# The prologue reordered: statistics of x after the second fold, the bias spread by a product with ones, and the guard's maxima before the statistics of batch 1

## The reference, cut to what matters

```python
def reference(x, Wq, Wk, Wv, Wo, bo, w_freq_real, w_freq_imag, bias):   # x is (8, 512, 256) f32
    def ffn(x):                                   # fft, product with a 256x256 complex matrix, real part of ifft
        y = real(ifft(einsum('bnd,do->bno', fft(x), w_freq_real + 1j * w_freq_imag)))
        return y + bias
    def attn(x):                                  # 16 heads of 8, on the left 128 columns of x
        left = x[..., :128]
        q, k, v = left @ Wq.T, left @ Wk.T, left @ Wv.T
        att = softmax(q . k / 4)                  # per head, over the keys
        return (att . v) @ Wo.T + bo
    x = x + 0.5 * ffn(layernorm(x))
    x = x + attn(layernorm(x))
    x = x + 0.5 * ffn(layernorm(x))
    return x
```

## Time and profile before

| what | value |
|---|---|
| median of 3 runs | 324.44 us (323.96 to 325.45) |
| span of the profiled execution | 327.4 us |
| granted TensorE clock, mean of the span | 0.995 |
| TensorE (PE) busy | 299.8 us, 92% |
| ScalarE (ACT) busy | 259.0 us, 79% |
| VectorE (DVE) busy | 190.3 us, 58% |
| GpSimd (POOL) busy | 97.8 us, 30% |
| first exponential of batch 0 starts at | 33.04 us |

### The profile page before, as it was taken

One profiled execution on the slowest core, in us unless ns is written; L12 is line 12 of the kernel. 1 busy time (PEld: TensorE's weight loads), 2 busy tenths in 40 slices (PEclk: granted clock), 3 DMA queues, 4 the chain that ended last, 5 costly groups with the idle time before them and its releaser, 6 DMA issues.

```text
span 327.4 us, 8919 instructions
## 1 busy us (share of the span) xinstructions
PE 299.8 (92%) x3452; PEld 113.8 (35%) x3452; DVE 190.3 (58%) x550; ACT 259.0 (79%) x287; POOL 97.8 (30%) x112
## 2 busy tenths in 40 slices
PE   8598999879998998999997999799997999898995
PEld 5444333233333432343332433233332323222333
DVE  1587438446775676657763677467764743361254
ACT  2114988978897988998995989878997999899921
POOL 6554701212504053033604053223600250034004
PEclk9999999999999999999997999999999999999999
DMA  7834459629654857748652858649354466303002
GB/s 200 298 132 171 104 202 173 175 86 139 209 201 135 188 107 256 225 147 147 237 182 70 188 105 289 193 140 151 114 163 146 102 180 167 109 28 103 35 32 66
DMA packets 29892, 49.87 MB, mean 152 GB/s; under 512 B 3600, under 2 KB 16272, under 8 KB 28944
## 3 DMA queue, kind: packets, MB, share of 16 engines
q1 hardware_dynamic: 29152, 48.79, 53.3%
q10 hardware_dynamic: 688, 0.40, 0.7%
HBM read 31.34 MB, written 17.83 MB: 150 GB/s over the span
## 4 chain that ended last, share of the span: by engine, by line
PE 57%; DMA 19%; SPq 9%; DVE 6%; issue 5%; ACT 3%; POOL 1%; DVEq 0%; ACTq 0%
PE misc L715 21%; PE ot L819 21%; PE scores L803 11%; DMA q_scr<-qp 7%; SPq L399 7%; DMA leftT<-left_scr 5%; DMA QS<-q_scr 4%; ACT probs L665 3%; DMA x_in<-x 2%; PE scores L715 1%; PE misc L689 1%; DVE stats L928 1%; DVE qp L972 1%; PE scores L682 1%; POOL rstd L547 1%
## 5 line engine op out<-in xcount | busy, mean ns | idle before, releaser
L665 ACT ACTIVATE probs<-scores 128x1024 f32<-128x1024 f32 x256 | 244.0, 1030 | 33.2 <-PE scores L803 33.0
L819 PE MATMUL ot<-probs,VS 128*32 128x512 f32 x1024 | 134.9, 598 | 4.8 <-ACT probs L665 3.4
L803 PE MATMUL scores<-QS,KS 32*128 32x512 f32 x512 | 65.0, 497 | 3.2 <-DMA QS<-q_scr 2.2
L803 PEld LDWEIGHTS scores<-QS,KS 32*128 32x128 f32 x512 | 24.6, 182 | 111.3 <-ACT probs L665 100.7
L819 PEld LDWEIGHTS ot<-probs,VS 128*32 128x32 f32 x1024 | 30.9, 110 | 28.4 <-ACT probs L665 7.7
L560 POOL TENSOR_TENSOR x_out<-x,half_bias 128x512 f32<-128x512 f32 x7 | 9.0, 1289 | 102.6 <-DVE x L1001 102.6
L1006 DVE SCALAR_TENSOR_TENSOR x_out<-misc,rstd,x_out 128x256 f32<-128x256 f32 x28 | 13.6, 484 | 38.7 <-PE misc L715 33.8
L545 POOL TENSOR_SCALAR veps<-mv 128x4 f32<-128x4 f32 (+1 forms) x25 | 5.9, 234 | 92.2 <-DVE mv L935 92.2
L715 PE MATMUL misc<-half_ffn,xT 128*32 128x256 f32 x448 | 32.1, 386 | 0.9 <-DMA xT<-x_scr 0.9
L715 PE MATMUL misc<-half_ffn,xT_in 128*32 128x256 f32 x400 | 27.7, 385 | 2.2 <-DVE half_ffn L1177 1.7
L547 POOL TENSOR_TENSOR rstd<-veps,power 128x4 f32<-128x4 f32 (+1 forms) x25 | 25.2, 1008 | 2.1
(11 more groups left out here) (126 smaller groups left out, 268.3 us busy)
## 6 DMA issues: line engine op xcount, KB each, us to landing
KS<-k_scr SPq DMA_DIRECT2D x56, 128.0 KB, 4.8
QS<-q_scr SPq DMA_DIRECT2D x56, 128.0 KB, 3.1
x_in<-x SPq DMA_DIRECT2D x8, 512.0 KB, 5.1
xT_in<-x_t SPq DMA_DIRECT2D x8, 512.0 KB, 6.5
k_scr<-kp SPq DMA_DIRECT2D x8, 512.0 KB, 2.7
q_scr<-qp SPq DMA_DIRECT2D x8, 512.0 KB, 4.6
x_scr<-x_blocks SPq DMA_DIRECT2D x7, 512.0 KB, 4.4
xT<-x_scr SPq DMA_DIRECT2D x7, 512.0 KB, 4.5
```

What stands on the lines that cost most here:

```text
L665: nc.scalar.activation(probs[u % PRING][:, :, :], scores[u % SRING][:, :, :], ACT.Exp, scale=SCORE_SCALE).then_inc(exp_done, 1)
L803: last = mm(scores[(u + j // 2) % SRING][:, j % 2, :], KS[b % 2][rows, slot, kt * P:(kt + 1) * P].bitcast(F32R), QS[b % 2][rows, slot, :]. ...
L819: last = mm(ot[COL * j:COL * (j + 1), :], VS[b % 2][:, kt, h, :], probs[(u + j // 2) % PRING][:, j % 2, :], start=s % 8 == 0, stop=s % 8 == 7)
```

## The change

The change touches only the prologue.

- VectorE: fold 2 no longer stands behind statistics of x. All four tiles' statistics of batch 0 come after fold 2; the memset of the cosine table's row comes right after fold 1.
- The bias is loaded first on ScalarE's queue, as one row of 256 into one partition. TensorE multiplies a row of 128 ones with it into a PSUM bank, ahead of piece 1. ScalarE makes `half_bias` from that bank, ahead of its copy of piece 1. The two tables are now second and third on ScalarE's queue.
- The fourth F1 of batch 1 is evacuated with the first three, ahead of KT and QT. The statistics and moments of batch 1 come after N and the chain that makes the flag, instead of between the evacuations and ahead of N.

```diff
-        jobs = [(f"F1_{t}", 1) for t in range(T)] + [("LT", 1)] + ahead[0:3] + [("KT", 1), ("QT", 1)] + ahead[3:4] + [("N", 1)]
+        jobs = [(f"F1_{t}", 1) for t in range(T)] + [("LT", 1)] + ahead + [("KT", 1), ("QT", 1), ("N", 1)]
...
-        bias_raw = sb("bias_raw", [P, E])
+        bias_raw = sb("bias_raw", [1, E])
+        ones_row = sb("ones_row", [1, P])
...
+        bias_bank = scores[2][:, 0, 0:E]
...
+            act.dma_start(bias_raw[:, :], bias.rearrange("(o e) -> o e", o=1)).then_inc(bias_loaded, 16)
             act.dma_start(cos_var_sb[:, :, :], cos_var.rearrange("(c p) e -> p c e", p=P)).then_inc(re_loaded, 16)
             act.dma_start(sin_sb[:, :, :], sin_tab.rearrange("(c p) e -> p c e", p=P)).then_inc(im_loaded, 16)
-            act.dma_start(bias_raw[:, :], bias.partition_broadcast(P)).then_inc(bias_loaded, 16)
...
+            act.wait_ge(bias_spread, 1)
+            nc.scalar.mul(half_bias[:, :], bias_bank, 0.5).then_inc(bias_set, 1)
             for piece, bank, copy in ((1, scores[0][:, 0], even[0]), (3, scores[1][:, 0], even[1])):
                 act.wait_ge(ffn_mm, piece)
                 nc.scalar.copy(copy[:, :, :], half_bank(bank)).then_inc(ffn_copied, 1)
-            act.wait_ge(bias_loaded, 16)
-            nc.scalar.mul(half_bias[:, :], bias_raw[:, :], 0.5).then_inc(bias_set, 1)
...
             pe.wait_ge(waking_set, 1)
             keep_awake(9)
+            pe.wait_ge(ones_set, 1)
+            pe.wait_ge(bias_loaded, 16)
+            mm(bias_bank, ones_row[:, :], bias_raw[:, :], start=True, stop=True).then_inc(bias_spread, 1)
             pe.wait_ge(re_loaded, 32)
...
             nc.vector.memset(waking[:, :].bitcast(I32), 0).then_inc(waking_set, 1)
+            nc.vector.memset(ones_row[:, :], 1.0).then_inc(ones_set, 1)
             nc.vector.memset(norms[:, :], 0.0).then_inc(norms_set, 1)
             fold(are_t, even[0], half_bank(scores[0][:, 1]), ALU.add, ALU.subtract, 2, 1)
-            norm0_stats(0, range(0, 2))
-
             dve.wait_ge(ffn_mm, 3)
             nc.vector.memset(cos_var_sb[0:1, 0, :], 1.0).then_inc(row0_set, 1)
             fold(aim_t, even[1], half_bank(scores[1][:, 1]), ALU.subtract, ALU.add, 4, 2)
-            norm0_stats(0, range(2, T))
+            norm0_stats(0)
             norm_moments(0, 1)
...
-            for s in range(T, T + 6):
-                run_jobs(PROLOGUE, s)
+            run_jobs(PROLOGUE, T)
+            for t in range(T):
+                evacuate(f"F1_{t}", 1)
+            run_jobs(PROLOGUE, 2 * T + 1)
+            run_jobs(PROLOGUE, 2 * T + 2)
             dve.wait_ge(row_ready, 1)
             nc.vector.tensor_copy(KS[0][:, 0, :].bitcast(F32R), row_banks[0]).then_inc(first_k_set, 1)
-            run_jobs(PROLOGUE, T + 6)
-            run_jobs(PROLOGUE, T + 7)
+            run_jobs(PROLOGUE, 2 * T + 3)
+            dve.wait_ge(evacuated, evac_count(f"F1_{T - 1}", 1))
+            for t in range(T):
+                norm_stats(1, x1[1], t, t == T - 1)
+            norm_moments(1, 2)
             guard(0)
```

More of the change, by code:

```diff
@@ L300, in build_macaron @@
         consts_set = sem("consts_set")
+        ones_set = sem("ones_set")
+        bias_spread = sem("bias_spread")
         bias_set = sem("bias_set")
```

## The result

The changed kernel is slower: 328.18 us median against 325.37 of the kernel before (20 runs each), ratio 1.0091 with a 95% interval of 1.0065 to 1.0118. A second comparison on another chip gave 1.0129 (1.0060 to 1.0198). The forecast was 322.2 us, a gain.

What follows compares the result with a forecast made beforehand. The body was taken as bound by a train of exponentials (244.0 of 327.4 us), only its start movable. Matrix stretch 1.95 - 0.9 = 1.05 plus guard stretch 1.14 gave 2.2 us: 324.44 - 2.2 = 322.2 us, range 321.0 to 324.2.

Steps and rivals of the forecast that it cites:

- D: Matrix stretch: delay of piece 4 by the bias product and later table issue, 0.9 us, leaving 1.95 - D as gain.
- The slower rival: ScalarE's queue: sine table lands 9.6 us after issue, at 11.4; D is 5.9, total 327.2 us; chance 0.08.
- The first rival: Engines serve 8 packets of x first: sine table lands at 7.4, D is 2.0, total 323.3 us; chance 0.12.
- The product: TensorE ahead of piece 1: the one-row bias product takes 0.45 us for 256 columns, a source of piece 4's delay.
- The 1.59 us of x: Matrix stretch: wait between pieces 4 and 5 for x and its first statistics, 1.59 us, expected to go.
- The 0.2 us to spare: Ahead of fold 3: VectorE's way with four statistics takes 2.5 us against TensorE's 2.68, so they are covered.
- The 0.36 us of fold 3: Matrix stretch: fold 3's first half gets 0.36 us shorter, as GpSimd's sum would be over earlier.
- The guard stretch: TensorE's flag load and branch move under the nine products of zeros, gaining the whole idle 1.14 us.
- the last rival: Batch borders in the body: if transfers don't follow, the gain is given back, 324.4 us; chance 0.09.

Runs made afterwards that it cites:

- after_again: The changed kernel, unchanged, for a second profile and timing on another chip; ratio 1.0129 against the kernel before.
- x_behind_tables: The changed kernel with x issued by SyncE only once wim and the sine table have landed; ratio 0.9981 against the kernel before.
- row_first_only: The kernel before with a load of one bias row, which nothing reads, put ahead of the tables on ScalarE's queue; ratio 1.0099 against it.
- guard_alone: The kernel before with only batch 1's job list, evacuation order and statistics place as changed; ratio 0.9973 against it.
- before_again: The kernel before, unchanged, for a second profile; F1 at 13.47 us, first exponential at 32.67, no ratio given.
- stats_guard: The kernel before with both VectorE reorderings and the bias left as a broadcast third on ScalarE's queue; 321.38 us against 323.06, ratio 0.9951.
- sin_on_sp: The changed kernel with the sine table's load moved to SyncE's queue, behind wim and ahead of x; ratio 0.9986 against the kernel before.
- bias_alone: The kernel before with only the bias part: row first, product ahead of piece 1, half_bias from PSUM; ratio 1.0150 against it.

## Why the prediction was wrong

- **The step that failed is D**, the delay of piece 4, taken as 0.9 us between the bounds 0.5 and 3.6. In the first profile it measured 4.82 us for piece 2's start and 2.06 more in pieces 2 to 4, 6.9 in all; in after_again 8.95 - 5.47 = 3.5, with none in the pieces. The upper bound was too low as well: it took x's landing as the latest at which the table could come, and the table landed at 10.25, after x (7.9) and after the transposed x (9.4), and in after_again at 8.91, after x (7.4). In place of two or three of x's packets in front of the table's last ones the runs show that about half of the tables' packets (272 of some 545 on that queue) were still to go when x's came, and that they took 5.9 us beside x, where the last 122 took 0.9 without it.
- **The term was sized by the issue time.** The sum treated "one place later" as 0.5 us of delay, with two or three of x's packets. x_behind_tables shows that 0.5 us of later issue is nothing alone (the table landed at 5.3), and row_first_only that the same 0.5 us beside x is 3.4 us of landing (8.8 instead of 5.4). A transfer without slack that loses its place to a large one doesn't lose the difference of the issue times.
- **The slower rival was the right one in kind.** It let the third transfer of the queue land 9.6 us after its issue; it was 8.5, and forecast 327.2 us against 328.18 measured (325.37 before). It was given 0.08, on the ground that the bias's packets were long and the table's short. That was beside the point: the long packets in the way were x's. That its loss of 2.8 us is the measured one is luck in part: its D of 5.9 has no clock in it, and D was 6.9 in one profile and 3.5 in the other.
- **The first rival**, the table behind a whole share of x, was too small: it put the table at 7.4 and the time at 323.3 us. Its mechanism is left open. The Trainium skill, "DMA: Bandwidth & Descriptors", Queues, rings and completion order, has an engine drain a group of descriptors of one ring before it switches. The counts in slices (35 and 4, later 17 and 79) come in bursts, which doesn't speak against it, but they can't show the order within one engine.
- **The clock was left out.** The prologue's idle times had cost no clock before, and the forecast never asked what a longer one would do. In the first profile the slow pieces are 2.06 of 4.19 us; in after_again there was none of it, with an idle time of 2.60 us.
- **The product** was put at 0.45 us and took 0.69 (0.62 on the chain), with piece 1 at 5.58 instead of 4.46; part of that is that the products of zeros ended later.
- **The 1.59 us of x** were right for that execution: the gap was 1.37 in the second profile and 0 in guard_alone, where x landed at 7.8, and it is gone wherever the statistics stand behind fold 2. **The 0.2 us to spare** for the four statistics were not there: in the changed kernel the chain goes through them, from fold 2 at 15.51 to fold 3 at 18.05. **The 0.36 us of fold 3** were no gain to count on: the first half took 0.43 us in before_again too, where the bias also came by the broadcast.
- **The guard stretch** was right: 1.14 forecast, 1.21 measured alone. One detail was wrong without consequence: the flag's first load takes 482 ns also where VectorE's comes later, so the 487 ns in the kernel before were no meeting of the two. In the changed kernel 0.83 us are left between F1 and the first exponential. In all kernels with the bias product VectorE's split of the queries starts 0.5 us after ScalarE's cast is done, against 0.1 in those without:

```profile
31.46 0.69 DVE L980 TENSOR_TENSOR qp<-scores,qp 128x512 fp32r<-128x512 f32 x1 [0.58 <-ACT qp L643]
```

  (the changed kernel; nothing in the trace accounts for the time, and it stays open).
- **The body** is not settled. stats_guard's 1.7 us of time stand beside 2.6 to 3.0 us of earlier first exponential, guard_alone's 0.9 beside 2.4 to 2.8, sin_on_sp's none beside 1.4 to 1.8, the changed kernel's 2.8 beside a later one by 0.6 to 4.6. So a part of a gain may be given back behind the prologue, which is the last rival. But each is from single profiles, and from the first exponential to the end these took 288.8 to 294.4 us in the kernels named here and the kernel before, too wide a spread to tell.

## What to carry to other kernels

A small transfer put at the head of a queue is not small for those behind it: ask what each of them will be queued beside on the shared engines, not only when it is issued, and take the worst landing in the profile as the price unless a run shows better. A load with no slack (here 0.04 us) does better in the ring ahead of the bulk that could overtake it: in sin_on_sp it landed at 6.4 us instead of 8.9 or 10.2. And a change that bundles a gain with a risk is worth splitting: here the two reorderings alone gave 0.5%, and the bias part cost 1.4 to 1.8%.

## What the runs showed of the hardware that was not expected

- Of two queues on the same 16 engines the one with packets of 4 KB moved 1.02 MB in 3.6 us, the one with packets of 516 bytes 0.12 MB. Its last 21 packets took more than 2 us, while the other queue moved 800.
- A one-row load of 1 KB ahead of two 129 KB tables went with a landing of the second table at 8.8 to 10.2 us instead of 5.4 to 5.7, in all five profiles (of three kernels) where x wasn't held back and the table stayed on that queue (bias_alone's, 9.8, left aside).
- At the start pieces of four products took 2.09, 1.93 or 1.06 us by execution, with the granted clock at 1.00 in the rows of x_behind_tables and row_first_only where they were slow. The granted clock doesn't tell all of TensorE's rate in the first 10 us. The nine products of zeros at the start tell the same: 3.45 to 4.02 us by execution at a granted clock of 1.00, against 1.96 for nine in the guard.
- TensorE's flag load began 1.0 us before the last of the nine products ahead of it in the stream had started (guard_alone).
